# An attention, expert and mixing layer on one core: the expert units planned with a lag of four pairs

## What is computed

```
x = x + attention(layernorm(x))     # 16 heads, l2-normed q, k, v; relu(q k)^2 v; tanh-normed output; @ Wout
x = x + experts(layernorm(x))       # 32 experts, 64 wide, top 8 of 4 of 8 groups, and one shared expert
x = x + taps(layernorm(x))          # per sequence of 512 tokens: softmax over 32 taps, out[l] = sum_d w[l,d] x[l+d]
x = x + experts(layernorm(x))       # the same weights again

# one expert block
scores = sigmoid(flat @ gate_w.T);  combine = normalised top-8 scores within the best 4 groups, else 0
out = sum_e combine[:, e] * ((silu(flat @ wg_e.T) * (flat @ wu_e.T)) @ wd_e.T)
out = out + (silu(flat @ sg.T) * (flat @ su.T)) @ sd.T
```

## Time and profile before

| | us |
|---|---|
| median of three runs | 638.05 |
| the profiled execution | 633.02 |
| its span, first to last instruction | 631.1 |
| PE busy in the span | 553.1 |
| DVE, ACT, POOL busy | 419.0, 377.9, 339.6 |
| attention, until the first silu of unit 0 | 242.7 |
| units 0 to 7, from first silu to first silu | 56.9, 48.3, 52.0, 49.6, 53.3, 45.4, 39.0, 43.9 |

### The profile page before, as it was taken

The page is one execution under the profiler, slowest core; times in us unless marked ns, Lnnn a source line. Parts: engine busy times, 40 slices in busy tenths (PEclk is TensorE's granted clock), DMA queues, the critical chain, the costliest instruction groups (busy, mean ns, idle before and its releaser), DMA issues.

```text
span 631.1 us, 10214 instructions
## 1 busy us (share of the span) xinstructions
PE 553.1 (88%) x3336; PEld 412.4 (65%) x3336; DVE 419.0 (66%) x993; ACT 377.9 (60%) x681; POOL 339.6 (54%) x286
## 2 busy tenths in 40 slices
PE   4498899999999886899897797997989799899996
PEld 3365667666676654777675576775767667677773
DVE  4756978787786694577385585476458457667663
ACT  5577867768686862445455653754744564655553
POOL 1634936657393730855365465454544554565664
PEclk9789989999999997999899998999989889999999
DMA  8100000000000019200925803911920860670920
GB/s 243 42 12 15 20 14 16 19 14 15 15 20 14 14 25 214 53 2 4 215 54 117 158 23 78 194 24 33 210 56 1 162 133 19 127 160 13 216 63 17
DMA packets 35204, 44.84 MB, mean 71 GB/s; under 512 B 4880, under 2 KB 18256, under 8 KB 35152
## 3 DMA queue, kind: packets, MB, share of 16 engines
q1 hardware_dynamic: 30736, 42.62, 31.4%
q10 hardware_dynamic: 4416, 1.57, 1.1%
HBM read 41.04 MB, written 3.15 MB: 70 GB/s over the span
## 4 chain that ended last, share of the span: by engine, by line
POOL 25%; issue 21%; PE 4%; DMA 1%; DVE 1%; POOLq 1%; ACT 0%; SPq 0%; DVEq 0%; ACTq 0%
POOL hl L463 20%; PE PS L1131 4%; POOL hls L467 1%; DMA wbc<-w_dram 1%; POOL fxl L427 1%; POOL rstd L420 1%; POOL mrstd L453 1%; POOLq L139 0%; DMA w_dram<-wTs 0%; DVE hb L1020 0%; DVE PS L1016 0%; POOLq L147 0%; ACT oT L678 0%; POOL ve L417 0%; POOL nmean L418 0%
## 5 line engine op out<-in xcount | busy, mean ns | idle before, releaser
L463 POOL TENSOR_TENSOR hl<-hb,hh 128x512 fp32r<-128x512 f32 x128 | 165.1, 1290 | 178.4 <-ACT hh L669 178.0
L662 ACT ACTIVATE sil<-PS 128x512 f32<-128x512 f32 (+1 forms) x136 | 81.2, 597 | 153.0 <-PE PS L1131 145.9
L1016 DVE TENSOR_TENSOR PS<-sil,PS 128x512 f32<-128x512 f32 x128 | 88.7, 693 | 113.6 <-PE PS L1131 74.9
L1131 PE MATMUL PS<-fxh,wfh 128*128 128x512 f32 x264 | 107.5, 407 | 2.3 <-issue 1.7
L1131 PE MATMUL PS<-fxl,wfh 128*128 128x512 f32 x264 | 106.8, 405 | 0.0
L1131 PE MATMUL PS<-fxh,wfl 128*128 128x512 f32 x264 | 106.3, 403 | 0.0
L1020 DVE TENSOR_TENSOR hb<-PS,wbc 128x512 f32<-128x512 f32 x128 | 88.5, 692 | 10.6 <-DMA wbc<-w_dram 6.2
L669 ACT ACTIVATE hh<-hb 128x512 fp32r<-128x512 f32 x128 | 79.8, 623 | 6.3 <-DVE hb L1020 6.1
L821 DVE SCALAR_TENSOR_TENSOR aT<-PS,rl 128x1024 f32<-128x1024 f32 x64 | 75.2, 1217 | 7.3 <-ACT rl L526 7.3
L1131 PE MATMUL PS<-hh,wfh 128*128 128x512 f32 x128 | 58.8, 460 | 20.9 <-POOL hl L463 14.3
L526 ACT ACTIVATE rl<-PS 128x1024 f32<-128x1024 f32 x64 | 62.4, 1033 | 18.3 <-PE PS L1131 17.9
(11 more groups left out here) (166 smaller groups left out, 935.1 us busy)
## 6 DMA issues: line engine op xcount, KB each, us to landing
wbc<-w_dram SPq DMA_DIRECT2D x64, 512.0 KB, 12.2
wfs<-wf_dram SPq DMA_DIRECT2D x32, 98.0 KB, 2.0
band_dram<-zero SPq DMA_DIRECT2D x16, 80.0 KB, 1.7
band<-band_dram ACTq DMA_DIRECT2D x4, 320.0 KB, 3.0
out_dram<-X SPq DMA_DIRECT2D x4, 256.0 KB, 2.3
X<-x_dram SPq DMA_DIRECT2D x1, 896.0 KB, 8.0
Osb<-wa_dram SPq DMA_DIRECT2D x1, 768.0 KB, 5.4
Osb<-wa_dram SPq DMA_DIRECT2D x1, 512.0 KB, 4.0
```

The costliest lines, as they stand in the source:

```text
L463: g.tensor_tensor(hl[:, n % RING, :], hb[:, n % RING, :], hh[:, n % RING, :].bitcast(F32), ALU.subtract).then_inc(F("hl"), 1)
L662: s.activation(sil[0:rows, n % 2, :], PS[0:rows, G0 + n % 2, :], ACT.Silu).then_inc(F("silu"), 1)
L1016: v_.tensor_tensor(PS[:, bank, :], sil[:, n % 2, :], PS[:, bank, :], ALU.mult).then_inc(F("t"), 1)
L1131: return nc.tensor.matmul(o, w, m, start=start, stop=stop)
```

## The change

1. `LAG` goes from 3 to 4 and `RING` from 4 to 5. On ACT `keep_sum` moves from behind the silu of pair 2 to ahead of that of pair 3.
2. The shared down product is two products. The high part `sd` is now loaded and copied into both halves of the contraction (128 partitions), and `hhs` holds the high part in its lower 64 partitions and the low part in its upper 64; so one product gives high times high plus high times low, the other low times high. The low part is made by DVE (`shared_low`, pair 0 of the next unit), no longer by POOL, and has its own semaphore `hls`.
3. Mixing: the normalised chunk is made in two halves in pairs 15 and 16 of unit `c+1`; its transposes, copy and logits move to pairs 0 and 2 of unit `c+2`. The steps behind them move two or three pairs later (put from 2 to 5, get from 5 to 8, bands from 8 to 11, apply from 11 to 13). `prep_normalise` of unit `u+1` is made in two halves in pairs 0 and 1 of unit `u`, no longer in pair 15 of the unit ahead.
4. The combine weights come back in six parts (`PARTS`): pair 0, pair 1, pairs 2 and 3, and then four pairs each; 12 DMAs for one unit in place of 8.
5. The end of attention: in unit 0 `scale_output(B-2, 2)` and `(B-2, 3)` stand ahead of the loop, the square roots of the output norms of batch 7 are two POOL instructions in pairs 2 and 5, and the last factors, spreads and projections move later, to pairs 8 to 16. In the batches, `values(n, 1, 0)` stands ahead of `transpose_norms`, and the routing of unit 0 is spread over batches 4 to 7.

The lines between that a reader needs least are left out:

```diff
-LAG = 3
-RING = 4
+LAG = 4
+RING = 5
+PARTS = (0, 1, 2, 4, 8, 12, NE)
...
@@ attention_turns
-        order += late(r, ("F", r, 2), ("F", r, 3)) + ([("pl", 0)] if b == B - 1 else [])
+        order += late(r, ("F", r, 2), ("F", r, 3))
         order += coming(n, ("qk", n, 0), ("qk", n, 1), ("v", n, 0, 0), ("v", n, 0, 1)) + late(q, ("nb", q))
-        order += late(q, ("nt", q)) + coming(n, ("v", n, 1, 0), ("v", n, 1, 1)) + late(r, ("y", r, 0))
+        order += coming(n, ("v", n, 1, 0)) + late(q, ("nt", q)) + coming(n, ("v", n, 1, 1))
...
+        def low_of(n):
+            u, p = divmod(n, NP)
+            return (F("hl"), u * NE + p + 1) if p < NE else (F("hls"), u + 1)
...
@@ SP, spread_weights
-                for k in range(4):
-                    if u == 0 and k == 3:
+                for k in range(len(PARTS) - 1):
+                    a, b = PARTS[k], PARTS[k + 1]
+                    if u == 0 and b == NE:
                         sp.wait_ge(cs("wfl"), PIECES)
                     for m in range(2):
-                        sp.dma_start(wbc[u % 2][m * I:(m + 1) * I, 4 * k:4 * k + 4, :],
-                                     rows[m, 4 * k:4 * k + 4, :].partition_broadcast(I)).then_inc(F(f"bc{k}"), 16)
+                        sp.dma_start(wbc[u % 2][m * I:(m + 1) * I, a:b, :],
+                                     rows[m, a:b, :].partition_broadcast(I)).then_inc(F(f"bc{k}"), 16)
...
@@ POOL
+            def last_output_norms(it):
+                q = B - 1
+                pool.wait_ge(*freed("nt", q))
+                signal = A("sr") if it else A("sr_half")
+                g.tensor_tensor(sr[:, it, :], n2o[:, it, :], half[:, 0:1].to_broadcast([P, H]), ALU.pow).then_inc(signal, 1)
...
-                else:
-                    after(pool, F("dn"), pair(u - 1, NE) + 1)
-                    g.tensor_tensor(hls[0:I, :], hb[0:I, n % RING, :], hhs[0:I, :].bitcast(F32),
-                                    ALU.subtract).then_inc(F("hl"), 1)
...
-                        output_norms(B - 1)
-                    if p == (3 if u else 5) and u + 1 < NU:
+                        last_output_norms(0)
+                    if u == 0 and p == 5:
+                        last_output_norms(1)
+                    if u == 0 and p == 6:
+                        last_output_scales()
+                    if p == (3 if u else 4) and u + 1 < NU:
                         prep_low(u + 1)
...
@@ ACT, expert units
+                    if p == LAG - 1 and u:
+                        keep_sum(u - 1)
                     gate(u, p)
...
-                    if p == 2 and u:
-                        keep_sum(u - 1)
+                    if 2 <= u < NC + 2 and p == 0:
+                        mix_tokens(u - 2)
                     if u + 1 < NU:
-                        if p == (4 if first else 2):
+                        if p in (0, 1) and not first:
+                            prep_normalise(u + 1, range(p * CT // 2, (p + 1) * CT // 2))
+                        if p == (3 if first else 2):
                             prep_tokens(u + 1)
...
-                        if p == 1:
+                        if p == 3:
                             mix_exp(u - 2)
-                        if p == 2:
+                        if p == 5:
                             mix_put(u - 2)
-                        if p == 5:
+                        if p == 8:
                             mix_get(u - 2)
-                        if p == 9:
+                        if p == 12:
                             mix_band(u - 2)
-                    if 1 <= u <= NC:
-                        if p == 13:
-                            mix_normalise(u - 1)
-                        if p == 15:
-                            mix_tokens(u - 1)
-                    if p == 15 and u + 2 < NU:
-                        prep_normalise(u + 2)
+                    if 1 <= u <= NC and p in (15, 16):
+                        mix_normalise(u - 1, range((p - 15) * CT // 2, (p - 14) * CT // 2))
...
@@ DVE, expert units
+            def shared_low(u):
+                dve.wait_ge(F("hh"), pair(u, NE) + 1)
+                v_.tensor_tensor(hhs[I:P, :], hb[0:I, pair(u, NE) % RING, :], hhs[0:I, :].bitcast(F32),
+                                 ALU.subtract).then_inc(F("hls"), 1)
...
+            scale_output(B - 2, 2)
+            scale_output(B - 2, 3)
             for u in range(NU):
                 first = u == 0
                 for p in range(NP):
                     hidden(u, p)
+                    if p == 0 and u:
+                        shared_low(u - 1)
...
@@ PE, attention
                 score(NG * b + 2)
+                if more:
+                    values(n, 1, 0)
                 if b:
                     transpose_norms(q)
                 if more:
-                    values(n, 1, 0)
                     values(n, 1, 1)
...
@@ PE, down
-                    split3(PS[:, D0, :], wfh[:, cols], wfl[:, cols], hhs[:, :], hls[:, :],
-                           start=False, stop=True).then_inc(F("dn"), 1)
+                    mm(PS[:, D0, :], wfh[:, cols], hhs[:, :], False, False)
+                    mm(PS[:, D0, :], wfl[:, cols], hhs[:, :], False, True).then_inc(F("dn"), 1)
...
@@ PE, expert units
+                    if 2 <= u < NC + 2 and p == 0:
+                        mix_transpose(u - 2)
                     if u + 1 < NU:
-                        if p == (3 if first else 1):
+                        if p == (3 if first else 2):
                             prep_transpose(u + 1)
...
                     if 2 <= u < NC + 2:
-                        if p == 8:
+                        if p == 2:
+                            mix_logits(u - 2)
+                        if p == 11:
                             mix_bands(u - 2)
                             mix_halo(u - 2)
-                        if p == 11:
+                        if p == 13:
                             mix_apply(u - 2)
```

More of the change, by code:

```diff
@@ L114, in expert_turns @@
         if 2 <= u < NC + 2:
+            turns.add(W1, "mx", u - 2)
+            turns.add(W1, "ml", u - 2)
             turns.add(W1, "mb", u - 2)
@@ L317, in _ @@
             sp.dma_start(bb[:, :], bb_in.partition_broadcast(P)).then_inc(ld("in_bb"), 16)
-            sp.dma_start(sdr[:, :], sd_in).then_inc(ld("in_sd"), 16)
+            for m in range(2):
+                sp.dma_start(sdr[m * I:(m + 1) * I, :], sd_in).then_inc(ld("in_sd"), 16)
             def weight_piece(k):
@@ L480, in _ @@
                         mix_deviation(u - 1)
-                    if p == 13 and u + 2 < NU:
+                    if p == 14 and u + 2 < NU:
                         prep_deviation(u + 2)
@@ L561, in prep_normalise @@
                     act.wait_ge(*full("px", u - 1))
-                for t in range(CT):
+                for t in tiles:
                     s.activation(xnp[:, t, :], Xt((u % NC) * CT + t), ACT.Identity, bias=shift[:, t:t + 1],
@@ L604, in _ @@
                 relu(NG * b + 1)
-                if last:
-                    prep_scores(0)
                 if more:
@@ L627, in _ @@
                 if b == B - 2:
-                    prep_normalise(0)
+                    prep_tokens(0)
+                if last:
+                    prep_weights(0)
                 relu(NG * b + 3)
@@ L633, in _ @@
                     keep_group(n, 1)
-                if last:
-                    prep_weights(0)
                 keep_output(NG * b + 2)
@@ L977, in _ @@
                     clear_norms(n, 0)
[L978 removed]
+                if b == B - 4:
                     prep_stats(0)
[L980 to L983 removed]
                 if more:
@@ L1017, in hidden @@
                     dve.wait_ge(F("t"), u * NE + p + 1)
-                    dve.wait_ge(F(f"bc{p // 4}"), 32 * (u + 1))
-                    after(dve, F("hl"), n - RING + 1)
+                    part = next(k for k in range(len(PARTS) - 1) if p < PARTS[k + 1])
+                    dve.wait_ge(F(f"bc{part}"), 32 * (u + 1))
+                    after(dve, *low_of(n - RING))
                     v_.tensor_tensor(hb[:, n % RING, :], PS[:, bank, :], wbc[u % 2][:, p, :], ALU.mult).then_inc(F("h"), 1)
                 else:
-                    after(dve, F("hl"), n - RING + 1)
+                    after(dve, *low_of(n - RING))
                     v_.tensor_tensor(hb[0:I, n % RING, :], sil[0:I, n % 2, :], PS[I:P, G0 + n % 2, :],
                                      ALU.mult).then_inc(F("h"), 1)
+            def shared_low(u):
+                dve.wait_ge(F("hh"), pair(u, NE) + 1)
+                v_.tensor_tensor(hhs[I:P, :], hb[0:I, pair(u, NE) % RING, :], hhs[0:I, :].bitcast(F32),
+                                 ALU.subtract).then_inc(F("hls"), 1)
             def add_experts(u):
@@ L1121, in _ @@
                         add_experts(u - 1)
-                    if p == 11 and 1 <= u <= NC:
+                    if p == 12 and 1 <= u <= NC:
                         mix_stats(u - 1)
```

(5 more changed lines are left out.)

130 lines of the change are left out of this document (60 added, 70 removed).

## The result

Four runs of the changed kernel have a median of 580.71 us (580.54 to 580.83), beside 637.43 (633.43 to 638.06, four runs) for the kernel before. The ratio of the two kernels' times is 0.9122, with a 95% interval of 0.9084 to 0.916. The profiled execution takes 580.82 us with a span of 579.0, where that of before took 633.02 with 631.1: 52.2 us less.

What follows compares the result with a forecast made beforehand. PE was taken as the bound, its idle time and slow clock as what could be won. Terms summed to 48.9 us off 633.0, giving 584.1; 3 to 5 us added for scatter made 588.0, range 577 to 606.

Steps and rivals of the forecast that it cites:

- The mixing hop: Mixing block: with more pairs for the trip, PE's waits for `xnm` go; 13.8 us (bounds 8 and 13.8).
- The sum's copy: Unit ends: ACT's copy ahead of pair 3's silu removes five PE waits for `oT`; 6.5 us (bounds 5 and 6.5).
- The lag: Expert pairs: four pairs from gate_up to down remove most `hl` waits; 11.3 of 14.3 us (bounds 7 and 13).
- Unit 0: Start of unit 0: scaling steps moved first on DVE cut PE's 4.1 us wait for `OTs` to 0.6; 3.5 us.
- Six parts: Combine weights: a smaller first part lands sooner in unit 1, removing PE's direct wait; 0.6 us (0 to 0.6).
- Shared down: Shared down product: one product less per unit, low part made by DVE in 0.69 us; 1.9 us.
- What comes with each wait: PE: 0.15 us more lost per wait, 22 waits gone, plus short weight-load stops; 5.0 us (bounds 2 and 8).
- The clock: Units 0 to 5: fewer half-speed windows, two left in units 1 to 5, one in unit 0; 8.4 us (3 to 12).
- Attention: Attention batches: products moved ahead of transpose_norms gain only in batch 1, `X` waits elsewhere; 0.9 us (bounds 0 and 5.4).
- New cost: Units 2 to 5, pairs 3 to 5: ACT's crowded queue rubs; 3.0 us charged (0 to 10).
- The first: Rival in attention: it gains too and nothing rubs, no wait for `X`, 4.5 + 3.0 us more, 580.5 us; chance 0.10.
- The one with ACT's queue: Rival in units 2 to 5: crowded pairs 3 to 5 on ACT reach PE, costing 16.4 us, 604 us; chance 0.15.

Runs made afterwards that it cites:

- the two moves: Changed kernel with ACT's copy of values(n, 1, 0) ahead of the squares, 580.15 us; then also DVE's first add_attention ahead of group 3's squares, 574.19 us.

## Why the prediction was right, and where it was off

It said 588.0 us, 577 to 606, and faster. The time is 580.71. Of its signs, those for the units came: no wait for `xnm`, 1.8 us for `oT` and `hl` together, units 2 to 5 at 42.1 to 42.7 us, no wait for a silu or an up bank. Term by term, as the sum puts them:

- **The mixing hop**, 13.8: all gone. In pair 0 PE makes the transposes 0.42 us behind the product ahead of them, where a product follows another after 0.23; the profile records no wait:

```profile
372.24 0.39 PE L1150 MATMUL PS<-fxh,wfl 128*128 128x512 f32 x1
372.66 0.66 PE L1406 MATMUL PS<-ident,xnm 128*128 128x128 f32 x4
```

The run with the hop undone adds that its part of the new kernel is 8.9 us, for the reason above.
- **The sum's copy**, 6.5: gone. The step was right. I priced it apart from the lag, but the runs show two ways to the same 6.5 us: the longer lag alone takes the `oT` waits away and brings 8.9 us of `fxh` waits in their place; the rest of the change, with a lag of three, takes them away and brings none of `fxh`.
- **The lag**, 11.3: 13.2. The wait that is left, 1.1 us, is the one at the end of the last unit. No crowded pair was left over. But 5.3 us came back as the waits for `bs` and `Fpad`, which a lag of three does not have. ACT is as late as I expected, by its idle time even later, but in pairs from which it no longer reaches PE; this is the silu behind the four issues, with 3.15 us of idle time before it against the 2.52 of the earlier trace rows:

```profile
345.39 1.83 ACTq L709 DMA_DIRECT2D band_dram<-wS  x4
347.32 0.60 ACT L679 ACTIVATE sil<-PS 128x512 f32<-128x512 f32 x1 [3.15 <-PE PS L1150]
```

- **Unit 0**, 3.5: 3.2. 0.86 us of the wait for `OTs` are left.
- **Six parts**, 0.6: 0.6 in direct wait, but the part is worth 6.1 us in the changed kernel. The step that failed is its bound, "0 to 0.6": I priced the DMA's lateness against `xnp` where it stood before, though I had moved it on ACT's queue myself in the same prediction. The parts of 128 KB landed after 2.9 us in the median; DVE waited 0.96 us for the first:

```profile
wbc<-w_dram SPq DMA_DIRECT2D x32, 128.0 KB, 2.9
...
294.84 0.69 DVE L1034 TENSOR_TENSOR hb<-PS,wbc 128x512 f32<-128x512 f32 x1 [0.96 <-DMA wbc<-w_dram]
```

- **Shared down**, 1.9: PE has 3328 products where it had 3336. `shared_low` took 0.69 us, as priced. The one exception is in the last unit, the only one of eight in which it started beside a POOL step: it began at 572.28, the POOL step ran until 572.72, and it took 0.99, 0.30 more. I had bounded it at 1.3 more. The Trainium skill's rule of an exclusive port pair (SBUF — State Buffer, "SBUF: two separate sides") says that such a step waits for all of the other's; the trace agrees in kind, but 0.30 is less than the 0.44 that were left of the POOL step.
- **What comes with each wait**, 5.0: by difference about 7.7. With the other terms as measured, 13.8 + 6.5 + 13.2 + 3.2 + 0.6 + 1.9, the clock below, 0.2 of attention and 5.3 of new waits, 44.5 of the 52.2 are accounted for. I have not taken this term apart. Of the 5.0, the 22 waits at 0.15 give 3.3; for the short stops of the weight loads no row gave a size, and no run shows one.
- **The clock**, 8.4: 10.4, by the price of the prediction and not measured by itself. In units 1 to 5 not one slow window is left, where I kept two. At the start of unit 0, where I forecast one, two are left, and in them PE is busy for 5.93 us, where in the three of before it was for 6.1; nothing was won there.
- **Attention**, 0.9: 0.2. That the three products would gain next to nothing was the right reading; that the wait would go to `X` was half of it. It went to `v` first, and `X` stood behind that, as the two moves showed. The sign that I gave, waits of about 0.9 us on `X`, did not come; the longest is 0.6.
- **New cost**, 3.0: 5.3 us of waits for `bs` and `Fpad`. The size is near, the place is not: I looked at ACT's queue in pairs 3 to 5, where nothing reached PE, and not at the bank `MB`, which the halo and the combine transposes share in neighbouring pairs, nor at DVE, which the longer lag leaves further behind PE.

That gives 52.2 where the sum had 48.9; the two agree this well in part by luck, since the 7.7 is a remainder and several terms erred in opposite ways. The shared product, the moves in unit 0 and the sum's copy were not undone one by one; their terms rest on the waits and counts in the profile. The larger error came behind the sum. I added 3 to 5 us because the runs of before lie above their profile by 5.0. The runs of the changed kernel lie on theirs, 580.54 to 580.83 beside 580.82; in the later set they lie up to 2.9 above it (577.91 to 580.82, the profile at 577.91). The addition was an argument about scatter and not a reading of a row; without it the forecast would have been 584.1.

Of the rivals, none came by its mechanism. The first named 580.5, which is almost the time measured, for attention gaining 4.5 us and nothing rubbing; attention gained 0.2, and 5.3 us rub. That its number fits is chance. The one with ACT's queue had its late silu, but not its effect. The broadcasts do not set the pace: DMA shares of 0.5 to 0.6 stand beside units that run at PE's pace.

## What to carry to other kernels

When a step waits in the middle of a round trip through several engines, count the pairs between the request and the need, and give the trip more of them; but an engine that no longer stops reaches its other waits earlier, so look at every copy that it asks of a busy in-order queue and move that too, or the gain comes back as another wait. A stall that is filled with work gains nothing if the bank that the engine wants next is freed by a third engine at a fixed time: look for the small instruction that frees it and move that. And price each move against the queues as they stand after all the other moves, not before.

## What the runs showed of the hardware

The same idle time can bring a slow clock or not. In two executions of the changed kernel PE has the same waits of 1.7 and 0.86 us at the start of unit 0 and is busy for the same 5.93 us in the same stretch. In the first it makes 29 of its instructions there, at a clock share of 0.50, in the second 48, at 1.00:

```profile
242.80:249.60 6.80, 5.93 (x29) 3.38 (x28) 3.74 (x12) 1.79 (x4) 0.00 (x0) 0.50 1.08 217
```

```profile
242.80:249.60 6.80, 5.93 (x48) 4.75 (x49) 5.31 (x15) 1.85 (x4) 2.26 (x4) 1.00 1.04 250
```

Unit 0 takes 49.9 us in the one and 47.3 in the other, which is most of the difference between their spans, 579.0 and 576.1. Nor does the length of one wait decide it. A slow window of 3.4 us followed the wait of 3.43 in unit 1 with the hop undone, and one of 6.8 a wait of 5.11 with four parts. But in the kernel before the same wait of 3.43 in unit 1 brought none, while those of 3.4 to 3.5 us in units 2, 3 and 4 did. The wait, and the stretch behind it:

```profile
340.59 0.66 PE L1386 MATMUL PS<-ident,xnm 128*128 128x128 f32 x4 [3.43 <-ACT xnm L685]
```

```profile
340.60:344.00 3.40, 3.40 (x17) 2.85 (x18) 1.94 (x3) 2.25 (x5) 2.23 (x4) 1.00 1.05 202
```

And 22 waits of up to 1.7 us, 13.3 in all, brought none with the lag undone, though in the kernel before slow windows followed waits of 1.61 us (ending at 309.42) and 1.20 (at 510.71), while waits of 1.28 (at 356.49) and 1.68 (at 362.36) were followed by none. So for a plan with waits of 1 to 3.5 us the clock is a matter of some luck, and it is one thing behind the scatter of a kernel's times that its profile alone does not tell.
